# Differential attention, first phase: all products on four 32-column tiles, and another order of the max pieces

## The reference, cut to what matters

```python
q1, q2, k1, k2 = (_heads(x, W, HS) for W in (Wq1, Wq2, Wk1, Wk2))   # 16 channels a head
v = _heads(x, Wv, 2 * HS)
att1 = softmax(where(mask, einsum('bhqd,bhkd->bhqk', q1, k1) * scale, -inf))
att2 = softmax(where(mask, einsum('bhqd,bhkd->bhqk', q2, k2) * scale, -inf))
y = einsum('bhqk,bhkd->bhqd', att1 - lam * att2, v)
# group norm of y over time, output projection Wc, x + ..., layer norm
```

## Time and profile before

| | |
|---|---|
| median of 3 runs | 6537.95 us (6537.2 to 6538.77) |
| the profiled execution | 6540.39 us, its span 6538.3 us |
| TensorE (PE) | 6038.8 us, 92% of the span, 33920 records |
| VectorE (DVE) | 4158.6 us, 64% |
| ScalarE (ACT) | 3490.1 us, 53% |
| GpSimd (POOL) | 874.3 us, 13% |
| mean granted clock | 0.975 |
| chain that ended last | PE 71%, DVE 12%, ACT 8%, issue 7%, DMA 2% |

### The profile page before, as it was taken

The page is one execution under the profiler, slowest core; times in us unless marked ns, Lnnn a source line. Parts: engine busy times, 40 slices in busy tenths (PEclk is TensorE's granted clock), DMA queues, the critical chain, the costliest instruction groups (busy, mean ns, idle before and its releaser), DMA issues.

```text
span 6538.3 us, 98212 instructions
## 1 busy us (share of the span) xinstructions
PE 6038.8 (92%) x33920; PEld 2589.0 (40%) x33920; DVE 4158.6 (64%) x10780; ACT 3490.1 (53%) x6980; POOL 874.3 (13%) x1873
## 2 busy tenths in 40 slices
PE   8999999999999999997899999999999999999985
PEld 3333333333333333322444444444444444444432
DVE  5777777777777777774556565565566655656533
ACT  4666656565666656554454545545455444454432
POOL 2222222222222222211000000000000000000000
PEclk9999999999999999998999999999999999999997
DMA  3223232232323232232000000000000000000004
GB/s 66 47 45 61 50 57 49 52 55 47 59 47 61 47 59 47 47 56 67 4 14 13 8 14 10 10 14 7 17 23 10 14 7 14 10 10 14 8 17 146
DMA packets 136941, 229.08 MB, mean 35 GB/s; under 512 B 40477, under 2 KB 40605, under 8 KB 135681
## 3 DMA queue, kind: packets, MB, share of 16 engines
q1 hardware_dynamic: 136448, 222.83, 16.6%
HBM read 53.86 MB, written 33.55 MB: 13 GB/s over the span
## 4 chain that ended last, share of the span: by engine, by line
PE 71%; DVE 12%; ACT 8%; issue 7%; DMA 2%; SPq 0%; POOL 0%; POOLq 0%; DVEq 0%; ACTq 0%
PE ps L673 15%; PE ps L766 9%; PE ps L637 8%; PE ps L881 6%; PE ps L656 6%; PE ps L906 4%; PE ps L817 4%; PE ps L856 3%; PE ps L563 3%; PE ps L837 2%; DVE mc L1370 2%; PE ps L825 2%; ACT sm L1183 2%; PE ps L584 2%; DVE junk L1366 2%
## 5 line engine op out<-in xcount | busy, mean ns | idle before, releaser
L1069 ACT ACTIVATE pt<-ps 128x1024 f32<-128x1024 f32 (+7 forms) x2048 | 1236.1, 652 | 866.4 <-PE ps L656 629.9
L1366 DVE CUSTOM_DVE_ANT_0 junk<-ps,causal 128x128 bf16<-128x128 f32 (+3 forms) x2048 | 989.5, 487 | 554.9 <-PE ps L637 536.8
L673 PE MATMUL ps<-pt,ones 128*32 128x512 f32 (+3 forms) x6144 | 1170.2, 495 | 0.0
L673 PE MATMUL ps<-pt,va 128*32 128x512 f32 (+3 forms) x3072 | 1164.2, 495 | 0.5 <-POOL pt L1736 0.4
L673 PE MATMUL ps<-pt,vs 128*32 128x512 f32 (+3 forms) x3072 | 1164.1, 495 | 0.0
L637 PE MATMUL ps<-kt,qt 96*128 96x512 bf16 (+3 forms) x3072 | 1019.7, 333 | 106.8 <-DVE mc L1370 56.7
L656 PE MATMUL ps<-qt,kt 98*128 98x512 bf16 (+3 forms) x3072 | 769.9, 328 | 26.6 <-ACT pt L1069 26.0
L1370 DVE TENSOR_REDUCE mc<-ps 128x1 f32<-128x512 f32 x1024 | 704.6, 688 | 90.8 <-PE ps L637 74.9
L766 PE MATMUL ps<-wqkv,xs 128*128 128x512 f32 x1536 | 740.1, 615 | 13.8 <-DMA wqkv<-in_wqkv 13.8
L1736 POOL TENSOR_SCALAR_AFFINE_SELECT pt<-pt 128x256 f32<-128x256 f32 x1024 | 448.3, 438 | 2269.6 <-ACT pt L1069 2269.6
L637 PEld LDWEIGHTS ps<-kt,qt 96*128 96x128 bf16 x3072 | 295.6, 96 | 1131.6 <-DVE mc L1366 635.1
(11 more groups left out here) (147 smaller groups left out, 8563.5 us busy)
## 6 DMA issues: line engine op xcount, KB each, us to landing
qt<-part SPq DMA_DIRECT2D x768, 64.0 KB, 2.4
kt<-part SPq DMA_DIRECT2D x768, 64.0 KB, 2.6
ya<-wy SPq DMA_DIRECT2D x128, 128.0 KB, 2.3
yb<-wy SPq DMA_DIRECT2D x128, 128.0 KB, 2.3
xs<-between_phases SPq DMA_DIRECT2D x32, 512.0 KB, 3.8
between_phases<-xo SPq DMA_DIRECT2D x32, 512.0 KB, 2.8
xt<-in_x SPq DMA_DIRECT2D x16, 512.0 KB, 6.0
between_phases<-z SPq DMA_DIRECT2D x16, 512.0 KB, 2.8
```

The costliest lines, as they stand in the source:

```text
L673: mmi = pe.matmul(ps[32 * q:32 * q + 32, 4 + half, lo - half * 512:hi - half * 512], w, probs(kb)[:, i, lo - first(kb):hi - first(kb)], st ...
L1069: act.activation(probs(kb)[:, i, kb * P - first(kb):1024 - first(kb)], ps[:, 2 * i:2 * i + 2, :].rearrange("p a q -> p (a q)")[:, kb * P:1 ...
L1366: ins = dve.tensor_tensor_reduce(out=junk[:, bank - 6, 0:w], in0=ps[:, bank, 0:w], in1=causal[:, 512 - w:512], scale=1.0, scalar=NEG, op0= ...
```

## The change

Every product of the first phase is now made by a helper that issues it four times, once for each tile of 32 columns of the weights, with the same moving operand:

```diff
+            def in_columns(bank, lo, hi, weights, moving, start, stop):
+
+                for q in range(4):
+                    mmi = pe.matmul(ps[32 * q:32 * q + 32, bank, lo:hi], weights[:, 32 * q:32 * q + 32], moving,
+                                    start=start, stop=stop)
+                return mmi
...
-                pe.matmul(ps[:, bank_of(slot), 0:w], qt[0:KDIM, u, i, r * P:(r + 1) * P],
-                          kt[0:KDIM, u, i, c0:c0 + w], start=True, stop=True).then_inc(max_full, 1)
+                in_columns(bank_of(slot), 0, w, qt[0:KDIM, u, i, r * P:(r + 1) * P],
+                           kt[0:KDIM, u, i, c0:c0 + w], True, True).then_inc(max_full, 1)
...
-                    mmi = pe.matmul(ps[:, 2 * i + half, lo - half * 512:hi - half * 512],
-                                    kt[0:KALL, u, i, kb * P:(kb + 1) * P], qt[0:KALL, u, i, lo:hi],
-                                    start=True, stop=True)
+                    mmi = in_columns(2 * i + half, lo - half * 512, hi - half * 512,
+                                     kt[0:KALL, u, i, kb * P:(kb + 1) * P], qt[0:KALL, u, i, lo:hi], True, True)
```

The same is done in `mean`, `variance`, `project_qk`, `project_v` and `project_out`. Values and the transpose stay as they are. The semaphore is counted up by the fourth product alone. Then the order on TensorE, and the places on VectorE:

```diff
                 next_scores(2, (1, 1))
-                weigh(1, (0, 1))
+                weigh(1, (1, 1))
                 next_scores(3, (1, 1))
-                weigh(2, (0, 1))
+                weigh(2, (1, 1))
                 next_scores(4, (1, 1))
                 unit(0)
-                weigh(3, (0, 1))
+                weigh(3, (1, 1))
                 next_scores(5, (0, 1))
                 unit(1)
+                weigh(4, (1,))
                 next_scores(6, (0, 1))
-                weigh(4, (0,))
                 weigh(5, (1,))
-                next_scores(7, (0, 2))
-                next_scores(8, (1, 1))
+                next_scores(7, (0, 0))
                 weigh(6, (0,))
+                next_scores(8, (0, 0))
                 weigh(7, (0,))
...
-                        if k == 13:
+                        if k == 15:
                             extra(g, 0)
-                        if k == 17:
+                        if k == 20:
                             extra(g, 1)
                         if h % 4 == 0 and g:
-                            if k == 15:
+                            if k == 13:
                                 sum_group(g // 4 - 1)
```

More of the change, by code:

```diff
@@ L547, in mean @@
                 for c in range(2):
-                    mmi = pe.matmul(ps[:, bank, :], mean_w[:], src[:, c, half * 512:half * 512 + 512],
-                                    start=c == 0, stop=c == 1)
+                    mmi = in_columns(bank, 0, 512, mean_w, src[:, c, half * 512:half * 512 + 512], c == 0, c == 1)
                 mmi.then_inc(mean_full, 1)
@@ L554, in variance @@
                 for c in range(2):
-                    mmi = pe.matmul(ps[:, bank, :], mean_w[:], rest[:, c, :], start=c == 0, stop=c == 1)
+                    mmi = in_columns(bank, 0, 512, mean_w, rest[:, c, :], c == 0, c == 1)
                 mmi.then_inc(var_full, 1)
@@ L562, in project_qk @@
                 for kc in kcs:
-                    mmi = pe.matmul(ps[:, bank, :], wqk[:, kc, n, c, :], xt[:, b % 2, kc, half * 512:half * 512 + 512],
-                                    start=kc == 0, stop=kc == 1)
+                    mmi = in_columns(bank, 0, 512, wqk[:, kc, n, c, :], xt[:, b % 2, kc, half * 512:half * 512 + 512],
+                                     kc == 0, kc == 1)
                 if kcs[-1] == 1:
@@ L573, in project_v @@
                     for kc in range(2):
-                        mmi = pe.matmul(ps[:, bank, blk * P:(blk + 1) * P],
-                                        xt[:, b % 2, kc, (4 * t + blk) * P:(4 * t + blk + 1) * P],
-                                        wv[:, kc, j * P:(j + 1) * P], start=kc == 0, stop=kc == 1)
+                        mmi = in_columns(bank, blk * P, (blk + 1) * P, xt[:, b % 2, kc, (4 * t + blk) * P:(4 * t + blk + 1) * P],
+                                         wv[:, kc, j * P:(j + 1) * P], kc == 0, kc == 1)
                 if blocks[-1] == 3:
@@ L583, in project_out @@
                     pe.wait_ge(yn_done, done(b * 4 + f + 1))
-                    mmi = pe.matmul(ps[:, bank, :], wc[:, f, oc * P:(oc + 1) * P],
-                                    ya[:, f, half * 512:half * 512 + 512], start=f == 0, stop=f == 3)
+                    mmi = in_columns(bank, 0, 512, wc[:, f, oc * P:(oc + 1) * P],
+                                     ya[:, f, half * 512:half * 512 + 512], f == 0, f == 3)
                 if fs[-1] == 3:
```

## The result

The changed kernel takes 6558.0 us (median of eight runs, 6553.5 to 6566.3) against 6537.4 for the kernel before (eight runs on the same chip): ratio 1.0033, interval 1.0022 to 1.0044. It is slower by 0.3%, which this measurement can just tell from no change. The profiled execution has a span of 6555.9 us, 17.6 more than the one of before.

The account below looks back on a forecast made before the run. TensorE was taken to bound the first phase. Tile changes would go but waits replace them; head kinds +25, -8, -10, +6 and narrow steps +13 gave +26, 6540.4 to 6566, hence 6564 as median; range 6420 to 6700.

Parts of the forecast that it names:

- Tile changes, 1.7 us a head: TensorE's changes between 128-column and 32-column products: removed, 218 us over 128 heads, 6320 with nothing else.
- the rival that gives the gap to the type: Gaps at data type changes: eleven bursts replace seven, nothing removed, 0.8 us a head added, 6640 to 6900; chance 0.05.
- Issue, 0.1 a head: Issuing four 32-column loads and products for each 128-column one on TensorE: costs 0.1 us a head.
- rival 6700 to 6860: Issue or load bound: narrow TensorE steps take 0.21 us, adding 160 to 320 us; chance 0.12.
- Waits of a head, 3.9: TensorE's waits under the new order, at pieces, first scores, block 1's scores and block 0's values: 3.9 us a head.
- Small gaps, 0.1: Small TensorE gaps in a head with query or key units: they take it from 22.7 to 22.8 us.
- the narrow steps' 13 us in all: TensorE's narrow steps, through the issue of more instructions: 13 us added over the kernel.
- The four kinds of heads: Heads with query or key units +25 us, values -8, without units -10, output products, means or variances +6.
- VectorE in every fourth head: Rival: affine and statistics work after pieces 9 and 20 delays pieces 12 and 23 over 1 us, 6630; chance 0.08.
- Phase two is not touched: The second phase: no change from the edit, nothing added to the sum.
- the wait at piece 9: TensorE waits 0.95 us a head there for piece 7's bank, freed after VectorE's normalisation.
- the waits are covered after all: Rival: waits at pieces 9, 13, 18 vanish; 6320 with waits as now, 6460 with half the growth; chance 0.30.

Follow-up runs that it names:

- experiments 1 and 2: 1: the 32-column tiles with the old order and VectorE places, 6408.9 us; 2: the kernel before with only the new order and places, 6738.0 us.
- experiment 5: Changed kernel with projections, output products, means and variances back on 128 columns: 6699.5 us, ratio 1.025.
- experiments 3, 6, 9: Changed kernel, moving: 3, normalisation to before piece 14, moved sum behind 18, 6510.4 us; 6, unit 0's residual behind piece 16, 6532.6; 9, ScalarE's copy earlier, 6550.7.
- balanced: Changed kernel with piece 9 behind block 2's first values, last two pieces behind the next head's first scores, residuals behind pieces 13 and 18: 6411.0 us, ratio 0.980.
- combined_residual: combined with ScalarE's copy after block 5's exponentials and the second residual in front of piece 20: 6317.8 us, ratio 0.966.
- combined: Changed kernel with normalisation before piece 13, residual 0 behind 16, moved sum behind 18, and pieces reordered: 6372.3 us, ratio 0.974.
- norm_late: Changed kernel with VectorE's normalisation moved from before piece 7 to before piece 14, moved sum behind piece 18: 6510.4 us, ratio 0.996.
- order_alone: Kernel before, on 128-column products, with only the new order and VectorE's new places: 6738.0 us, ratio 1.030.

## Why the prediction was right, point by point

Sign, time and range hold: 6558.0 against 6564, inside 6420 to 6700. The mechanism is the one foretold, and experiments 1 and 2 show its two halves. That the two times lie 6 us apart is in part luck, as the sum at the end of this list shows.

- **Tile changes, 1.7 us a head.** Right. No gap is left, float32 to bfloat16 on 32 columns has a median under 10 ns, so the rival that gives the gap to the type falls, and experiment 5 buys gaps back at 0.10 to 0.12 each, with another 0.107 for the load that the entry leaves uncovered.
- **Issue, 0.1 a head; rival 6700 to 6860.** Right: 6 ns at a narrow step, and loads of 94 ns run beside the products. The rule of the Trainium skill weighed in the prediction ("TensorEngine Tiling (Array Packing)", "Restrictions", and the load by columns over 1.2 GHz) does not show in the time here: by it a 128-column step would take an estimated 0.107 us, it takes 0.06.
- **Waits of a head, 3.9.** 3.7 in the trace, by places: piece 9 0.95 as said; piece 13 0.49 (0.48 said); piece 18 0.50 (0.62); next first scores 0.33 (0.46); block 1's scores 0.66 and 0.47 (0.60 and 0.48); piece 5 0.10 and piece 6 none (0.2 said for both); block 0's values 0.08 (0.1); and 0.10 before block 6's values, not said. The 1.8 us of waits that the prediction gives the kernel before are, by this count, 1.5 of waits and some 0.35 of small gaps. The causes of pieces 9 and 18 and of the first scores are shown by taking each away (experiments 3, 6, 9); those of piece 13 and of block 1 only by the releasers in the trace and by balanced, which moved several things at once.
- **Small gaps, 0.1 and the narrow steps' 13 us in all.** Undersized for the head: 1 to 13 ns at some 80 steps are about 0.5 us. With 18.8 and 3.7 that is the measured 22.96, against 22.8.
- **The four kinds of heads.** From transpose to transpose, after less before, each stretch sorted by the units whose products stand in it:

| heads | predicted each, sum | measured each, sum |
|---|---|---|
| 56 with query or key units | +0.45, +25 | +0.47, +26 (0.60 in half, 0.48 and 0.17 in a quarter each) |
| 28 with values units | -0.29, -8 | -0.04, -1 (0.06 to 0.17 in three of four, -0.70 in most of the fourth) |
| 14 without units, and the first stretch | -0.6, -10 for 16 | -13 and -1.2 (-0.36 in half, up to -2.3) |
| 28 with output products, means, variances | +0.2, +6 | +0.61, +17 (1.47, 0.73, 1.07, -0.84) |
| narrow steps, in all | +13 | in the rows above |

The sum to the last transpose is 27.8 against 26, and 28.4 with the start: right as a whole, by terms that missed on either side. The term for the 56 heads with query or key units is right to 1 us; the worst-sized one is the last kind, priced as one number where it is four. The rival "VectorE in every fourth head" is true at one place in it: in the head of 26.9 us piece 12 waits 0.97 more. In the head of 23.7 with the mean's products, 22.7 before, piece 18 waits 1.03 in place of 0.50 and piece 23 waits 0.47. Two other kinds with such work on VectorE got shorter (24.7 to 23.8, 23.1 to 22.4). Values heads were reckoned at 21.75 and are 22.20: the head with query units, from which they were reckoned, is 0.2 longer than said, the two waits that they lack are 0.50 and 0.33 and not 0.62 and 0.46, and small gaps add some 0.1 (422 records); that the first scores do not wait in them holds.
- **The end and the second phase.** Missing from the sum: the end has no pieces to wait for and is 4.1 us shorter, 1.7 of it by a higher granted clock. "Phase two is not touched" is right for the program; its time in the two profiled executions differs by 6.7 us all the same. So the 17.6 of the spans are 26 foretold, 1.8 and 0.6 more to the last transpose, 4.1 less in the end and 6.7 less in the second phase. The last term is luck.
- **What the wait at piece 9 hid.** Not seen. The mask beside the normalisation was late by 1.05 us already in the changed kernel, under the wait at piece 9; only balanced, which removed that wait, showed what it costs.

Of the rivals, "the waits are covered after all" was the one to fear, and its figure for waits as before (6320) is what combined_residual reaches by moving them away: the waits belonged to where the pieces and VectorE's work stood.

## What to carry to other kernels

A faster engine does not shorten a loop whose handoffs are placed for the slower one: tiles and order have to be changed together, and here 240 us lay between the order that came with the tiles (6558) and one that fits them (6318). Before work is moved to an engine's idle time, follow the chain through all engines: the copy that seemed to block ScalarE lay in time in which it waited for VectorE, and moving it gave nothing. When the time of a phase is compared between two traces, let both windows end at the same instruction, and look at what a phase that was not touched does from run to run. Price a wait also by what it covers, since the next one behind it comes to light when it goes.

## What the hardware showed unexpectedly

GpSimd's mask of 128x256 float32 takes 0.41 us, but 1.47 if it starts as VectorE begins its 1.22 us product of two SBUF operands. In the kernel before, the first mask of a head starts 1.35 us ahead of the normalisation; in the changed kernel 0.03 behind it. GpSimd in order of time, first the kernel before, where the next mask starts 0.92 into the normalisation:

```profile
1515.80 0.41 POOL L1736 TENSOR_SCALAR_AFFINE_SELECT pt<-pt 128x256 f32<-128x256 f32 x1 [2.46 <-ACT pt L1069]
1518.06 0.57 POOL L1736 TENSOR_SCALAR_AFFINE_SELECT pt<-pt 128x256 f32<-128x256 f32 x1 [1.86 <-ACT pt L1069]
```

then the changed one:

```profile
1533.23 1.46 POOL L1740 TENSOR_SCALAR_AFFINE_SELECT pt<-pt 128x256 f32<-128x256 f32 x1 [2.46 <-ACT pt L1073]
```

VectorE there:

```profile
1533.20 1.22 DVE L1395 TENSOR_TENSOR wy<-ev,wy 64x1024 f32<-64x1024 f32 x1
```

and all 1024 masks of that kernel (shortest, median, longest in ns):

```profile
L1740 POOL TENSOR_SCALAR_AFFINE_SELECT pt<-pt x1024: 400/406/1463, 89.5 to 3041.6; 128x256 f32<-128x256 f32 x171
```

Then combined, where a mask starts in the middle of a normalisation, GpSimd first and VectorE after it:

```profile
1446.06 1.06 POOL L1740 TENSOR_SCALAR_AFFINE_SELECT pt<-pt 128x256 f32<-128x256 f32 x1 [2.09 <-ACT pt L1073]
```

```profile
1445.63 1.22 DVE L1395 TENSOR_TENSOR wy<-ev,wy 64x1024 f32<-64x1024 f32 x1
```

In both the mask ends 0.27 us after VectorE's instruction does (1534.69 against 1534.42, 1447.12 against 1446.85), whenever it began, while VectorE's takes 1.22 either way. The 125 masks that start 0.92 into it in the kernel before take 0.57 and end at the same distance. So it does not run slower, it stands still. The other way round VectorE pays: in norm_late the mask starts first, 0.19 ahead of the normalisation of 1501.60,

```profile
1501.41 0.41 POOL L1740 TENSOR_SCALAR_AFFINE_SELECT pt<-pt 128x256 f32<-128x256 f32 x1 [2.09 <-ACT pt L1073]
```

and it is VectorE's instruction that takes 1.29 for 1.22; in order_alone, where the mask starts 0.06 ahead, it takes 1.42. The Trainium skill's page "SBUF — State Buffer", section "SBUF: two separate sides", states this as an exclusive lock on a port pair that GpSimd shares with VectorE, held by a VectorE instruction with two SBUF inputs; the traces agree, with 0.41 us becoming 1.47. That it is these two ports, and not something else the two engines share, no run here tells apart.
